# A fused linear-attention and slot-expert layer on one core: identity products, biases written to banks, smaller norms and new orders of phase 1

## The reference, cut to what matters

```python
# layer 1: linear attention, 16 heads of 8
x = x + attn(layernorm(x))
#   q', k' = exp(proj(q) - |q|^2/2), exp(proj(k) - |k|^2/2), per head of 8
#   kv = k'^T v per head;  z = 1 / (sum(q') + 1e-8);  out = (q' @ kv) * z @ Wo.T + bo
# layer 2: 16 slots read the sample, pass one expert each, and are read by the tokens
x = x + ffn(layernorm(x))
#   o = slot_query + mha(slot_query, x, x, ...d weights) + d_bo
#   h = layernorm(o, gain_e, shift_e)
#   u, g = silu(h @ W1_e + b1_e), silu(h @ Wg_e + bg_e);  y = (u * g) @ W2_e + b2_e
#   out = mha(x, o + y, o + y, ...c weights)
```

## Time and profile before

| what | value |
| --- | --- |
| time, median of 3 runs | 195.14 us (194.88 to 195.6) |
| the profiled execution's own time | 194.75 us |
| its span, first to last instruction | 193.0 us, 4707 instructions |
| PE busy | 179.7 us, 93% of the span |
| DVE, ACT, POOL busy | 141.6, 116.6, 146.3 us |
| HBM read, written | 15.84 MB, 2.10 MB |

### The profile page before, as it was taken

How to read it: one execution, slowest core, us unless ns; L and a number is a source line. 1 busy time by engine, 2 the same in 40 slices (tenths; PEclk the granted TensorE clock), 3 DMA queues, 4 the chain that set the end, 5 groups by cost and what they waited for, 6 DMA issues and landing times.

```text
span 193.0 us, 4707 instructions
## 1 busy us (share of the span) xinstructions
PE 179.7 (93%) x1439; PEld 136.6 (71%) x1439; DVE 141.6 (73%) x413; ACT 116.6 (60%) x296; POOL 146.3 (76%) x286
## 2 busy tenths in 40 slices
PE   0898789999999999999999999999999799999993
PEld 0445477777876687777788767523777699999993
DVE  2669968788877887869785743655448999999961
ACT  2235367796688857867966675446334465666561
POOL 4498969879699985999277693317947999999960
PEclk9999999999999999999999999999999999999999
DMA  4739957999990000000000000000000001111122
GB/s 108 240 102 366 360 147 257 349 362 327 372 298 13 0 3 2 3 0 3 0 3 0 2 5 0 3 0 0 3 0 0 3 27 54 58 58 54 38 75 82
DMA packets 19674, 18.24 MB, mean 95 GB/s; under 512 B 1289, under 2 KB 15458, under 8 KB 19650
## 3 DMA queue, kind: packets, MB, share of 16 engines
q1 hardware_dynamic: 18802, 17.35, 28.3%
q10 hardware_dynamic: 848, 0.59, 1.1%
HBM read 15.84 MB, written 2.10 MB: 93 GB/s over the span
## 4 chain that ended last, share of the span: by engine, by line
PE 80%; POOL 11%; DMA 3%; DVE 2%; issue 1%; ACTq 1%; ACT 1%; POOLq 0%; DVEq 0%
PE ps L1061 11%; PE ps L1133 7%; PE ps L1328 7%; PE ps L1300 7%; PE ps L1183 4%; PE ps L1171 4%; PE ps L1241 4%; PE ps L1114 4%; PE ps L1071 4%; PE ps L1318 4%; PE ps L1094 3%; PE ps L1309 3%; PE ps L1084 3%; DMA X<-in_L_attn_x_dram 3%; PE ps L1125 2%; PE ps L1104 2%
## 5 line engine op out<-in xcount | busy, mean ns | idle before, releaser
L1061 PE MATMUL ps<-Wproj,xnT 128*128 128x512 f32 x64 | 32.5, 633 | 0.9 <-ACT Wproj L515 0.5
L481 POOL TENSOR_TENSOR pr<-ft,rsm 128x256 f32<-128x256 f32 x32 | 19.3, 625 | 0.9 <-DVE rsm L970 0.9
L1061 PEld LDWEIGHTS ps<-Wproj,xnT 128*128 128x128 f32 x64 | 11.4, 198 | 9.9 <-issue 8.6
L1133 PE MATMUL ps<-XN2T,Ad 128*128 128x256 f32 x64 | 16.7, 384 | 0.1
L1328 PE MATMUL ps<-sq,prT 128*128 128x128 f32 x128 | 16.8, 275 | 0.0
L1300 PE MATMUL ps<-xnT,XN2T 128*128 128x256 f32 x64 | 16.5, 383 | 0.0
L429 POOL TENSOR_SCALAR xn<-X,nm,rs 128x127 f32<-128x127 f32 x32 | 14.7, 468 | 1.5
L1328 PEld LDWEIGHTS ps<-sq,prT 128*128 128x128 f32 x128 | 15.5, 192 | 0.0
L794 DVE TENSOR_REDUCE ss<-sq 128x64 f32<-128x512 f32 x16 | 10.9, 678 | 5.8 <-ACT sq L555 5.7
L654 ACT ACTIVATE ft<-ex 128x512 f32<-128x512 f32 x16 | 10.1, 630 | 8.3 <-POOL pr L481 7.1
L548 ACT ACTIVATE pr<-ps,nmax 128x256 f32<-128x256 f32 x32 | 14.9, 474 | 0.3 <-DVE nmax L833 0.2
(11 more groups left out here) (178 smaller groups left out, 508.6 us busy)
## 6 DMA issues: line engine op xcount, KB each, us to landing
W1s<-in_L_ffn_e_W_dram SPq DMA_DIRECT2D x4, 1024.0 KB, 8.0
Wgs<-in_L_ffn_e_Wg_dram SPq DMA_DIRECT2D x4, 1024.0 KB, 8.3
W2s<-in_L_ffn_e_W_dram SPq DMA_DIRECT2D x16, 256.0 KB, 8.3
out_dram<-V2s SPq DMA_DIRECT2D x16, 128.0 KB, 1.7
X<-in_L_attn_x_dram SPq DMA_DIRECT2D x3, 512.0 KB, 6.1
X<-in_L_attn_x_dram ACTq DMA_DIRECT2D x2, 128.0 KB, 2.6
X<-in_L_attn_x_dram ACTq DMA_DIRECT2D x1, 256.0 KB, 4.9
W<-in_L_ffn_e_b_dram SPq DMA_DIRECT2D x3, 32.0 KB, 1.8
```

The lines of the kernel that those rows point to most:

```text
L481: last = pool.tensor_tensor(heads(at[:, k, j * HS:(j + 1) * HS], S), heads(ep[:, k, j * HS:(j + 1) * HS], S), over(rsm[:, k, j * H:(j + 1) ...
L1061: last = pe.matmul(banks(b)[:, j, :], xnT[:, k, j * P:(j + 1) * P], Wproj[:, :], start=True, stop=True)
L1133: last = pe.matmul(ps[:, 4, hf * NT:(hf + 1) * NT], Ad[:, hf * P:(hf + 1) * P], XN2T[:, b, :], start=True, stop=True)
```

## The change

It does the following. (a) `warm(n)` multiplies the identity by itself n times on PE, into a bank that is overwritten later: five times before the bias rows, once each before the weights' transposes, behind them, and before the first projection. (b) The slots' residual is no longer four products: DVE adds a replicated slot query (a new load, `slotr`) and `d_bo` (now loaded on all 128 partitions) straight into banks 0 and 1, and PE's products go on top of it. `repS`, `slotb` and their steps on POOL and DVE are gone. (c) The biases of the last three inner products (group 2 gate, group 3 both) come as fp32 rows by twelve new loads (`hbias`), and ACT copies them into the banks; three of eight `hidden_bias` products go. (d) The norms subtract the mean instead of adding its negative, so POOL's multiplications by -1 go (in `rstd1` and `rstd2`, and for DVE's first norm). (e) `ft` has 9 columns per head, the ninth of which holds 1e-8 once and for all, so DVE's sum includes it and the addition goes; `ft` is written by ACT and read by POOL and by `key_sums` on PE with a hole behind each 8 values. (f) New orders of phase 1 on all four engines. (g) `QUERIES1` and `QUERIES2` fall by one: one query fewer ahead of the slots' projection, one more (13, 14, 15) behind step 3 of phase 2.

```diff
-QUERIES1 = 6
-QUERIES2 = 11
+QUERIES1 = 5
+QUERIES2 = 10
...
+        hbias = sb("hbias", P, 3, F)
-        d_bo_all = sb("d_bo_all", S, P)
+        d_bo_all = sb("d_bo_all", P, P)
+        slotr = sb("slotr", P, G, P)
-        ft = sb("ft", P, 2, 2, 2 * P)
+        ft = sb("ft", P, 2, 2, 2 * H, DH + 1)
...
+            for j in range(EG):
+                sp.dma_start(slotr[j * Q:(j + 1) * Q, :, :], slot.rearrange("o (g j) d -> j (o g) d", j=EG)[j]
+                             .unsqueeze(0).broadcast_to([Q, G, P])).then_inc(slots_in, 16)
+            for n, (g, v) in enumerate(((2, bg), (3, b1), (3, bg))):
+                for j in range(EG):
+                    e = g * EG + j
+                    sp.dma_start(hbias[j * Q:(j + 1) * Q, n, :], v[e:e + 1, :].broadcast_to([Q, F])).then_inc(h_in, 16)
...
+            pool.memset(ft[:, :, :, :, DH], 1e-8).then_inc(den_term, 1)
             def slot_rows():
-                own(pool.memset(repS[:, :, :], 0.0))
-                each = repS[:, :, :].rearrange("p g (j b) -> p (g j) b", b=Q)
-                own(pool.affine_select(out=each, in_=each, compare_op=ALU.not_equal, fill=1.0,
-                                       base=0, pattern=[[-1, S], [0, Q]], channel_multiplier=1))
                 own(pool.memset(aoT[:, :, :], 0.0))
...
-                pool.tensor_tensor(nm1[:, first:end, :], mv1[:, first:end, :, 0],
-                                   minus[:, 0:2 * n].rearrange("p (b j) -> p b j", j=2), ALU.mult)
...
-                                              nm1[:, b, j:j + 1], rs1[:, b, j:j + 1], ALU.add, ALU.mult)
+                                              mv1[:, b, j, 0:1], rs1[:, b, j:j + 1], ALU.subtract, ALU.mult)
...
-            rstd1(0); rstd1(1); apply1(1); rstd1(3); apply1(2); apply1(3); slot_rows(); other_masks(); add_bias(0)
-            add_bias(1); scale_features(0); add_bias(2); rstd1(5); scale_features(1); apply1(4); add_bias(3)
-            rstd1(7); rstd2(0); apply2(0); scale_features(2); apply1(5); rstd2(1); apply2(1); add_bias(4)
+            rstd1(0); rstd1(1); apply1(1); rstd1(3); apply1(2); slot_rows(); other_masks(); apply1(3)
+            scale_features(0); add_bias(0); rstd1(5); apply1(4); add_bias(1); scale_features(1); rstd2(0); apply2(0)
...
-                sc.activation(ft[:, b % 2], ex[:, b % 2], ACT.Exp).then_inc(ft_ok, 1)
+                sc.activation(ft[:, b % 2, :, :, 0:DH], ex[:, b % 2].rearrange("p j (h d) -> p j h d", d=DH),
+                              ACT.Exp).then_inc(ft_ok, 1)
...
+            def set_bias(n):
+                i = 5 + n
+                sc.wait_ge(sg_ok, i - 4)
+                sc.activation(ps[:, BANK_UP[i], :], hbias[:, n, :], ACT.Copy).then_inc(bias_set, 1)
+            sc.wait_ge(h_in, 16 * 3 * EG)
+            tanh(0, 0); tanh(0, 1); tanh(1, 0); set_bias(0); tanh(1, 1); set_bias(1); tanh(2, 0); set_bias(2)
+            tanh(2, 1); act_columns(0); tanh(3, 0); act_columns(1); tanh(3, 1); act_columns(2); act_columns(3)
...
+            def slots_residual():
+                ve.wait_ge(slots_in, 16 * EG)
+                ve.wait_ge(ex_ok, NB)
+                for half in range(2):
+                    last = ve.tensor_tensor(ps[:, half, 0:2 * P].rearrange("p (g d) -> p g d", g=2),
+                                            slotr[:, 2 * half:2 * half + 2, :], under(d_bo_all[:, :], 2), ALU.add)
+                last.then_inc(slots_set, 1)
...
-                ve.tensor_reduce(den[:, k, :].rearrange("p (j h) -> p j h", j=2),
-                                 ft[:, k, :, 0:P].rearrange("p j (h d) -> p j h d", d=DH), AX.X,
+                ve.tensor_reduce(den[:, k, :].rearrange("p (j h) -> p j h", j=2), ft[:, k, :, 0:H, :], AX.X,
                                  ALU.add).then_inc(den_ok, 1)
-                ve.tensor_scalar(den2[:, k, :], den[:, k, :], 1e-8, None, ALU.add).then_inc(den2_ok, 1)
...
-            stats1(0); moments1(0); center_weights(); set_biases(); apply_first(); spread_rotation(); stats1(1)
-            moments1(1); stats1(2); center_values(); moments1(2); stats1(3); moments1(3); stats1(4); stats1(5)
-            moments1(4); stats1(6); norms_sq(0); exponents(0); moments1(5); stats1(7); moments1(6); sums(0)
-            moments1(7); norms_sq(1); exponents(1); mask_kv(0); norms(0); sums(1); norms(1); norms_sq(2)
+            stats1(0); moments1(0); center_weights(); set_biases(); apply_first(); spread_rotation(); stats1(1)
+            moments1(1); stats1(2); stats1(3); moments1(2); moments1(3); stats1(4); stats1(5); center_values()
+            moments1(4); norms_sq(0); exponents(0); stats1(6); moments1(5); sums(0); stats1(7); norms(0)
+            norms_sq(1); exponents(1); mask_kv(0); norms_sq(2); exponents(2); center_slot_weights(); sums(1)
...
+            def warm(n):
+                pe.wait_ge(ident_ok, 1)
+                for _ in range(n):
+                    pe.matmul(ps[:, 2, 0:P], ident[:, :], ident[:, :], start=True, stop=True)
...
-                    last = pe.matmul(ps[:, 2, 3 * P:4 * P], xn[:, b % NX, j, :], ft[:, b % 2, j, P:2 * P],
+                    last = pe.matmul(ps[:, 2, 3 * P:4 * P], xn[:, b % NX, j, :], ft[:, b % 2, j, H:2 * H, 0:DH],
...
-            turn_biases(); turn_weights(); turn_xn(0); feature_weights(); project(0); turn_xn(1)
-            turn_value_weights(); project(1); key_sums(0); turn_xn(2); key_values(0); project(2)
+            warm(5); turn_biases(); warm(1); turn_weights(); warm(1); turn_xn(0); feature_weights(); warm(1)
+            project(0); turn_xn(1); turn_value_weights(); project(1); turn_xn(2); key_sums(0); project(2)
...
-            turn_pr(13); scores(14); slot_sums(2); slot_values(14); slots(13); turn_xn2(15); turn_pr(14); scores(15)
-            slots(14); queries(0); slot_values(15); queries(1); turn_pr(15); slot_sums(3); queries(2); slots(15)
-            queries(3); slot_sums(4); slots_residual(); queries(4); queries(5)
+            slot_sums(2); slots(13); turn_xn2(15); turn_pr(14); scores(15); slots(14); slot_values(15); queries(0)
+            queries(1); turn_pr(15); slot_sums(3); queries(2); slots(15); queries(3); slot_sums(4); queries(4)
             pe.wait_ge(ao_ok, len(POST))
             pe.wait_ge(w_rest, 16 * N_REST)
+            pe.wait_ge(slots_set, 1)
...
             def experts_in(g, u):
                 pe.wait_ge(hT_ok, 1 + g // 2)
+                wait(pe, bias_set, 2 * g + u - 4)
...
-            hidden_bias(2, 1); experts_in(2, 1); turn_act(0); hidden_bias(3, 0); experts_in(3, 0); turn_act(1)
-            hidden_bias(3, 1); experts_in(3, 1); experts_out(0); turn_act(2); experts_out(1); turn_act(3)
+            experts_in(2, 1); turn_act(0); experts_in(3, 0); turn_act(1); experts_in(3, 1); experts_out(0); turn_act(2); experts_out(1); turn_act(3)
```

More of the change, by code:

```diff
@@ L1032, in score_weights @@
                 pe.matmul(ps[:, 4, 0:HS], Wt[:, 0, :], qbd[:, :], start=True, stop=True).then_inc(su_pe, 1)
-            def slots_residual():
-                pe.wait_ge(post_masks_ok, 1)
-                pe.wait_ge(rows_ok, 1)
-                wait(pe, ex_ok, NB)
-                for g in range(G):
-                    pe.matmul(ps[:, g // 2, (g % 2) * P:(g % 2 + 1) * P], repS[:, g, :], slotb[:, :],
-                              start=(g % 2 == 0), stop=False, skip_group_check=True)
             def slot_sums(g):
@@ L1194, in _ @@
-            key_sums(6); turn_xn2(4); turn_pr(3); attention_out(5); turn_xn(8); slot_values(4); key_values(6)
-            scores(4); turn_qz(6); project(8); attention_out(6); turn_xn2(5); key_sums(7); turn_pr(4); turn_xn(9)
-            key_values(7); scores(5); turn_qz(7); slots(3); slot_values(5); project(9); slots(4); attention_out(7)
-            key_sums(8); turn_xn2(6); turn_pr(5); key_values(8); turn_xn(10); scores(6); slot_values(6); turn_qz(8)
-            slot_sums(0); project(10); slots(5); turn_xn2(7); key_sums(9); turn_pr(6); attention_out(8); scores(7)
@@ L1204, in _ @@
-            turn_qz(12); slot_values(10); slot_sums(1); turn_xn2(11); attention_out(12); key_sums(13); turn_xn(15)
-            turn_pr(10); scores(11); key_values(13); project(15); turn_qz(13); slots(9); slot_values(11)
-            attention_out(13); turn_xn2(12); key_sums(14); slots(10); key_values(14); turn_pr(11); scores(12)
-            turn_qz(14); slot_values(12); slots(11); attention_out(14); key_sums(15); turn_xn2(13); turn_pr(12)
-            key_values(15); scores(13); turn_qz(15); slots(12); slot_values(13); attention_out(15); turn_xn2(14)
@@ new lines, in _ @@
+            key_values(0); turn_slot_weights(); turn_qz(0); turn_xn(3); key_sums(1); attention_out(0); project(3)
+            slot_queries(); key_values(1); key_sums(2); turn_qz(1); score_weights(); turn_xn2(0); attention_out(1)
+            turn_xn(4); key_values(2); slot_values(0); scores(0); turn_qz(2); project(4); attention_out(2)
+            turn_xn2(1); key_sums(3); turn_pr(0); turn_xn(5); scores(1); slot_values(1); key_values(3); slots(0)
```

(16 more changed lines are left out.)

176 lines of the change are left out of this document (79 added, 97 removed).

## The result

The changed kernel takes 207.06 us (206.12 to 208.04, four runs) against 195.06 for the one before on the same chip: a ratio of 1.0606, interval 1.0572 to 1.064. It is **slower by 12.0 us** where 189.5 was forecast. Its profiled execution took 207.18 us, span 205.4.

What follows compares the result with a forecast made beforehand. PE was taken to bound the dense part, waits the start. Gains 4.0 + 1.1 - 0.3 + 0.8 = 5.6 off 194.75 gave 189.15, with the median's offset 189.5 us; range 187.6 to 193.3, the forecast's own 188.6 to 190.6.

Steps and rivals of the forecast that it cites:

- the start's sum for POOL: Before apply2(0) ends, POOL's queue loses repS, small multiplications, two bias additions and rstd1(7): together 5.0 us.
- Clock: At the start, identity products on PE bring project(0) from 3.78 to 1.98 us: 1.80 gained, at worst nothing.
- the prediction's rival with 0.17: The clock rises no earlier, project(0) keeps 3.78 us and the start gives 2.5, not 4.0: 191.0 us; chance 0.17.
- The knee: The point after turn_xn2(0) from which PE hardly waits comes 2.9 to 5.0 us sooner; 4.0 taken, identity products included.
- the prediction's third case: New orders give nothing at the start, DVE or ACT being late, or gaps open in the dense part: 193.5; chance 0.12.
- Slots' residual: At the end of phase 1, four products leave PE for two DVE additions: 1.08 us gained.
- The moved query: End of phase 1 and last loop: just no wait for aoT, at worst 0.3; up to 0.43 later; 0.3 net charged.
- Hidden biases: In the expert stretch, three of eight bf16 products leave PE for ACT copies: 0.8 us gained, bounds 0 and 0.93.
- The ninth column: Sixteen additions of 1e-8 leave DVE, whose sums read 9 values a head instead of 8: costed at nothing.
- The rival of strided features: Key sums on PE read features with holes; if that doubled their 64 records, 7.0 us more: 196.5; chance 0.06.
- The prediction's sign of trouble: In the dense part, fewer than 7.9 PE records per us between 30 and 90 would show the forecast wrong.
- the sign that it named for the forecast: At the start, project(0) at about 1.9 us would be among the signs showing the forecast right.

## Why the prediction was wrong

**The step that failed** is in the start's sum for POOL, "four multiplications by -1 of 0.19 each ... 0.6 after overlap". It priced what part (d) takes away and never what it puts in: the norm's subtracting form was carried at the old form's price without being said. No row of before shows that form, so it had to be bounded from both sides, and wasn't. The runs put 0.82 to 0.83 us in the place of 0.46, 62 times; by the two full kernels (207.06 less 190.11) it costs 16.95 us. What its removal of the multiplications gains is nothing that can be seen, where the sum had 0.6.

An estimate from rows of before would have shown the danger. Before, POOL was busy 86% of the dense part, where a sample takes 6.0 us (project(4) at 29.43, the projection four samples on at 53.43). So POOL has some 0.8 us to spare per sample, and there are four norms in it: 0.2 us more on each makes POOL the bound. At 0.36 each POOL needs 5.2 and 1.45, 6.6 us a sample, 0.6 more than PE's period. Over the some eleven samples of the dense part that is about 7 us lost. After, eleven samples took 77.9 us, from project(4) at 30.39 to project(15) at 108.28, 7.1 each; the other 0.5 was not taken apart; waits of POOL and PE for each other, as in the kernel with half of the slow norms, and the second stretch at half rate lie in it. So the estimate is too mild: with the second norms alone slow, POOL has 0.7 us more per sample, less than the 0.8 to spare, and yet 9.6 us were lost. Against the kernel with the old norms the 17.0 us between the spans lie so: 3.4 before project(4) (27.03 to 30.39), 12.2 from there to project(15) (65.7 to 77.9), 1.4 behind it.

**The other terms**, by the kernels with the old norms:

- Clock: forecast 1.80 whole, measured 1.85; right where both hold: the clock comes up, and POOL isn't what PE waits for next. "Nothing" was named as the lower bound without either condition. In the old order POOL makes it nothing, and in one of nine traces the clock stayed down, which is the prediction's rival with 0.17 and its reason, the gaps of PE ahead of project(0).
- The knee: forecast 4.0 sooner, 2.9 to 5.0 if all go along. With the negated means project(4) came 2.40 sooner, in the trace of the kernel that adds the mean 3.12, and in the run in which the clock stayed down 0.82. In the first of these POOL's queue had lost what was said, but for the multiplications; yet the load of the biases (0.56) and DVE's moments (0.74) became the last to end, in the way in which the prediction's third case has its suppliers late. The 1.44 us of `repS` that the sum took off POOL's queue showed no gain at the start.
- Slots' residual: 1.08 forecast, 1.06 measured. The moved query: no wait for aoT appeared, as forecast; DVE had it at 115.89 and PE took it at 116.07. Its other half, up to 0.43 in the last loop, was not tried alone.
- Hidden biases: 0.8 forecast, 0.83 by the medians, 0.75 by the trace.
- The ninth column: forecast at nothing, measured at nothing. The rival of strided features is refuted.

All parts but the norm give 4.98 together where 5.6 was forecast; 1.85, 1.06 and 0.83 make 3.7, and the 1.2 left, the orders of the start and the moved query, is a difference and was not measured by itself. The forecast less its failed step would have been near, 190.11 against 189.5, with the start too high and the products that left PE right. Of the rivals, the one on the slower side had 0.06 and another mechanism; none was the norm's new form.

**What would show it.** The prediction's sign of trouble, fewer than 7.9 PE records per us between 30 and 90, came true (6.5), and with it the waits behind POOL; the sign that it named for the forecast, project(0) at 1.9 us, came true as well and said nothing about the rest.

## What to carry to other kernels

When an edit swaps an operation inside an instruction that stays, give the new form a price and a bound of its own, also where the number of operands and elements is the same; the removed helper is the small part. On POOL, keep scalar pairs at those seen quick here, and keep a sign in the tile that holds the scalar, as the kernel before does: the small multiplication for it cost nothing that could be seen. Work out for each engine that isn't the bound how much longer its instructions may get before it is, per sample and not as a share of the whole: here it was 0.2 us on each of four. Take that as the point past which the loss is certain, not as room that is free: 0.36 us on two of the four already cost 9.6 us. And look at the clock of every run before a trace is taken for all of them.

## What was not expected of the hardware

POOL's instruction with two scalars costs between 449 and 842 ns at 127 columns by the pair of operations alone, and 554 against 1236 to 1244 ns at 256, while two-tensor forms cost the same for add, subtract and multiply, and the two pairs tried on DVE took the same. TensorE's clock, once up, came down again in the middle of a kernel behind waits of PE: 0.51 for 3.4 us twice in the trace of the changed kernel, 0.50 for 6.8 us in one run of ten of the old kernel with identity products. And the same program with the same identity products ran project(0) in 1.98 us in one trace and in 3.21 in another.
